# First routed layer: the up weights centred and split in two halves, ahead of the pages of the last two rounds, over four PSUM banks

## The reference, cut to what matters

```python
x = x + 0.5 * _L1_ffn_ref(_layernorm(x, axis=-1), L1_ffn_w_gate, L1_ffn_w_g, L1_ffn_w_u, L1_ffn_w_d)

def _L1_ffn_ref(x, w_gate, w_g, w_u, w_d):
    scores = x @ w_gate
    topk_scores, topk_idx = jax.lax.top_k(scores, K)
    topk_probs = jax.nn.softmax(topk_scores, axis=-1)
    gating = jnp.sum(jax.nn.one_hot(topk_idx, E, dtype=topk_probs.dtype) * topk_probs[..., None], axis=-2)
    hidden = jax.nn.silu(jnp.einsum('bsd,edm->ebsm', x, w_g)) * jnp.einsum('bsd,edm->ebsm', x, w_u)
    expert_out = jnp.einsum('ebsm,emd->ebsd', hidden, w_d)
    return jnp.einsum('bse,ebsd->bsd', gating, expert_out)
```

## Time and profile before

| | |
|---|---|
| median of 3 runs | 1740.12 us (1738.24 to 1742.35) |
| the profiled execution's own time | 1738.08 us |
| its span in the profile | 1735.6 us |
| mean granted TensorE clock | 0.884 of 2.4 GHz |
| busy, of the span | PE 84%, PEld 77%, DVE 76%, ACT 61%, POOL 62% |
| the first routed layer's rounds 2 and 3, arranging and up weights | about 838 to 909 us |
| its blocks | about 909 to 1115 us |

### The profile page before, as it was taken

How to read it: one execution, slowest core, us unless ns; L and a number is a source line. 1 busy time by engine, 2 the same in 40 slices (tenths; PEclk the granted TensorE clock), 3 DMA queues, 4 the chain that set the end, 5 groups by cost and what they waited for, 6 DMA issues and landing times.

```text
span 1735.6 us, 39578 instructions
## 1 busy us (share of the span) xinstructions
PE 1455.1 (84%) x10269; PEld 1333.8 (77%) x10269; DVE 1319.5 (76%) x4027; ACT 1053.3 (61%) x2639; POOL 1080.8 (62%) x1708
## 2 busy tenths in 40 slices
PE   8799999689948999998437999876999981289996
PEld 8589999667747999998316999875988861189995
DVE  7789999789988888888744777644788985367774
ACT  4588888444426888884214767574777730056674
POOL 7538887777733354533836666740788977746665
PEclk9999999899968999997567999955989975589998
DMA  6111010840001111002111222032222201122210
GB/s 195 50 38 32 32 35 13 190 111 1 0 6 55 35 33 36 31 8 107 46 52 47 67 64 54 20 105 64 86 74 78 82 15 47 56 62 65 65 51 9
DMA packets 93273, 96.25 MB, mean 55 GB/s; under 512 B 12072, under 2 KB 75709, under 8 KB 92576
## 3 DMA queue, kind: packets, MB, share of 16 engines
q1 hardware_dynamic: 83168, 76.70, 15.3%
q0 software_dynamic: 9920, 17.35, 3.0%
HBM read 63.75 MB, written 33.78 MB: 56 GB/s over the span
## 4 chain that ended last, share of the span: by engine, by line
PE 61%; issue 14%; DVE 12%; POOL 5%; ACT 4%; DMA 1%; another core or an unknown queue 1%; SPq 1%; DVEq 1%; POOLq 0%; ACTq 0%
PE banks L621 5%; PE banks L610 4%; PE banks L1300 4%; PE banks L1287 3%; PE banks L1322 3%; PE banks L1289 3%; PE banks L1288 3%; PE banks L601 3%; PE banks L603 3%; PE banks L602 3%; PE banks L1302 3%; PE banks L1301 3%; PE banks L622 2%; PE banks L1272 2%; PE banks L1273 1%
## 5 line engine op out<-in xcount | busy, mean ns | idle before, releaser
L1545 DVE TENSOR_TENSOR choice_hlo<-choice_h,choice_hhi 128x512 fp32r<-128x512 f32 x256 | 177.0, 732 | 22.8 <-ACT choice_hhi L1398 22.0
L1390 ACT ACTIVATE choice_h<-banks 128x512 f32<-128x512 f32 x256 | 152.4, 600 | 58.9 <-PE banks L1289 49.0
L892 DVE SCALAR_TENSOR_TENSOR top_h<-top_silu,top_xs,banks 128x176 f32<-128x176 f32 x364 | 128.5, 395 | 71.7 <-ACT top_silu L678 54.4
L933 POOL DMA_INDIRECT rt_rows<-X,top_slot x128 | 130.5, 1019 | 63.5 <-issue 37.8
L678 ACT ACTIVATE top_silu<-banks,top_xs 128x352 f32<-128x352 f32 x182 | 100.8, 554 | 102.7 <-PE banks L603 81.4
L1287 PE MATMUL banks<-choice_xin_hi,ec_w_hi 128*128 128x256 f32 x512 | 145.5, 284 | 4.8 <-ACT choice_xin_lo L1383 3.6
L1300 PE MATMUL banks<-choice_hhi,ec_w_hi 128*128 128x256 f32 x512 | 146.1, 285 | 3.4 <-DVE choice_hlo L1545 2.8
L1398 ACT ACTIVATE choice_hhi<-choice_h 128x512 fp32r<-128x512 f32 x256 | 146.6, 625 | 0.0
L1639 POOL TENSOR_SCALAR choice_y_hi_lo<-choice_yw 128x512 fp32r<-128x512 f32 x64 | 41.3, 645 | 164.9 <-ACT choice_yw L1413 163.8
L1288 PE MATMUL banks<-choice_xin_lo,ec_w_hi 128*128 128x256 f32 x512 | 143.6, 281 | 0.0
L1289 PE MATMUL banks<-choice_xin_hi,ec_w_lo 128*128 128x256 f32 x512 | 143.6, 280 | 0.0
(11 more groups left out here) (349 smaller groups left out, 5362.1 us busy)
## 6 DMA issues: line engine op xcount, KB each, us to landing
choice_token_row<-choice_tokens SPq DMA_DIRECT2D x64, 256.0 KB, 3.1
mlstm_run_row<-mlstm_run SPq DMA_DIRECT2D x32, 512.0 KB, 3.6
rt_rows<-rt_blank SPq DMA_DIRECT2D x2, 6188.0 KB, 38.3
top_xs<-rt_rows SPq DMA_DIRECT2D x182, 68.0 KB
X<-in_x SPq DMA_DIRECT2D x8, 512.0 KB, 6.9
ec_stage<-in_ec_w SPq DMA_DIRECT2D x2, 2048.0 KB, 12.8
X<-rt_y SPq DMA_DIRECT2D x8, 512.0 KB, 7.1
rt_rows<-X,top_slot POOLq DMA_INDIRECT x128
```

The costliest lines, as they stand in the source:

```text
L1545: dve.tensor_tensor(flat(self.hlo), self.h[:, c, :], flat(self.hhi).bitcast(F32), ALU.subtract).then_inc(self.hlo_done, 1)
```

## The change

The eight experts' chains are split into two halves and moved. TensorE computes experts 0 to 3 after the last scores and ahead of the ranks of round 2, and experts 4 to 7 behind those ranks and ahead of `arrange_sums`. ScalarE makes the high parts of experts 0 and 1 ahead of round 2's exponential and those of 2 to 7 behind it. VectorE makes the low parts of experts 0 to 3 behind round 2's `choose`, ahead of round 2's `page`, and those of 4 to 7 behind round 3's `choose`, ahead of round 3's `page`. There are four banks in place of two (6, 7, 0 and 1), so expert e waits for e-4.

```diff
-        self.pw = bk[6:8]
+        self.pw = (bk[6], bk[7], bk[0], bk[1])
...
         def centre_up(e):
             pe.wait_ge(w.split.loaded, 16 * (w.split.loads + len(w.parts)))
-            if e >= 2:
-                pe.wait_ge(sh.weights_lo, w.ups_from() + e - 1)
-            pe.matmul(self.pw[e % 2][:, 0:self.UP], w.centre[:, :], w.up[:, e, :], start=True, stop=True).then_inc(w.centred, 1)
+            need(pe, sh.weights_lo, w.ups_from() + e - 3 if e >= 4 else 0)
+            pe.matmul(self.pw[e % 4][:, 0:self.UP], w.centre[:, :], w.up[:, e, :], start=True, stop=True).then_inc(w.centred, 1)
 
         self.scores(pe, self.AHEAD[self.run], B)
         for r in range(self.CHOSEN_AHEAD[self.run], self.ROUNDS):
+            if not self.run and r == self.EARLY - 1:
+                for e in range(E // 2):
+                    centre_up(e)
             if r == self.EARLY:
+                if not self.run:
+                    for e in range(E // 2, E):
+                        centre_up(e)
                 self.arrange_sums(pe)
-                if not self.run:
-                    for e in range(E):
-                        centre_up(e)
             self.rank(pe, r)
...
+    def up_hi(self, act, first, last):
+        w = self.w
+        for e in range(first, last):
+            act.wait_ge(w.centred, e + 2)
+            act.activation(w.up_hi[:, e, :], self.pw[e % 4][:, 0:self.UP], ACT.Copy).then_inc(self.sh.weights_hi, 1)
+
+    def up_lo(self, dve, first, last):
+        sh, w = self.sh, self.w
+        for e in range(first, last):
+            dve.wait_ge(sh.weights_hi, w.ups_from() + e + 1)
+            dve.tensor_tensor(w.up_lo[:, e, :], self.pw[e % 4][:, 0:self.UP], w.up_hi[:, e, :].bitcast(F32),
+                              ALU.subtract).then_inc(sh.weights_lo, 1)
...
         for r in range(self.CHOSEN_AHEAD[self.run], self.ROUNDS):
-            if r == self.EARLY and not self.run:
-                for e in range(E):
-                    act.wait_ge(w.centred, e + 2)
-                    act.activation(w.up_hi[:, e, :], self.pw[e % 2][:, 0:self.UP], ACT.Copy).then_inc(self.sh.weights_hi, 1)
+            if not self.run and r == self.EARLY - 1:
+                self.up_hi(act, 0, 2)
             self.gate_exp(act, r)
+            if not self.run and r == self.EARLY - 1:
+                self.up_hi(act, 2, E)
...
-            if (r, part) == (self.EARLY, "choose") and not self.run:
-                for e in range(E):
-                    dve.wait_ge(sh.weights_hi, w.ups_from() + e + 1)
-                    dve.tensor_tensor(w.up_lo[:, e, :], self.pw[e % 2][:, 0:self.UP], w.up_hi[:, e, :].bitcast(F32),
-                                      ALU.subtract).then_inc(sh.weights_lo, 1)
+            if not self.run and (r, part) == (self.EARLY - 1, "page"):
+                self.up_lo(dve, 0, E // 2)
+            if not self.run and (r, part) == (self.EARLY, "page"):
+                self.up_lo(dve, E // 2, E)
             (self.choose_whole if part == "choose" else self.page)(dve, r)
```

## The result

The changed kernel takes 1730.99 us (median of 6 runs, 1725.16 to 1738.26) against 1740.88 us of the kernel before beside it (6 runs, 1730.85 to 1747.74). The ratio is 0.9941, with a 95% interval of 0.9914 to 0.9968: faster by 10 us, between 6 and 15. The forecast was 1728. Two later groups of runs, each beside the kernel before on one chip, gave the same kernel 0.9958 (0.9935 to 0.9982) and 0.9981 (0.9963 to 1.0000), so there is a gain, and it is rather 3 to 10 us than 12; the last of the three intervals just reaches no change. The profiled execution took 1730.98 us, its span is 1728.4 us (before: 1735.6).

A forecast was written before the change was run, and what follows sets the result against it. The stretch was taken as bound by a chain of waits, not a busy engine. Sends 18.9 us earlier, less a longer lag, gave 11.9 us off 1738.08, 1726.2; the median's 2.04 us above made it 1728, range 1719 to 1734.

The forecast's parts named there:

- Arranging to choice: VectorE's row between arranging and round 3's choice: the up weights' whole 19.78 us leave the path.
- First half: Experts 0 to 3, around round 2's ranks and page: ranks 0.9 us later, low parts hidden in VectorE's wait, ending at 856.3.
- the later 3.1 us of the old wait: VectorE's 5.19 us idle before round 2's page: ranks there after 2.1, the rest possibly with its own cause; 0.9 us charged.
- Second half: Experts 4 to 7, up to round 3's page: matmuls and high parts covered, low parts filling the ranks' wait, page at 882.9.
- a first send later than 895: Sign of being wrong at round 3's first send, forecast at 890.9: a later start would mean a pause on the path.
- What follows the sends: Last sends to seventh silu: sends end 18.9 us earlier at 910.8, silu at 927.0, 11.9 us earlier than before.
- the second layer's lag: Second routed layer: seventh silu 16.2 us after the last send, taken for the first layer in place of 9.2.
- the sum: Whole kernel: 11.9 us off the profiled 1738.08 us gives 1726.2, with a median forecast of 1728.
- The loads aren't held back: Rival, block loads beside the last sends: they go out unhindered, gaining 18.9 to 21.2 us, 1719 to 1721; chance 0.17.
- The pauses come along: Rival, ScalarE's high parts: 9.2 us of pauses fall on experts 0 to 3, leaving 2.7 us gained; chance 0.06.
- The slower rival: Block loads beside the sends starve at 5.7 us each, losing some 30 us, 1770; chance 0.03.

The follow-up runs named there:

- the hold in the kernel before: Kernel before, with GpSimd waiting ahead of round 2's fifth send until all eight low parts are there: 1734.13 us, ratio 0.9985.
- the sends paced: Changed kernel, with GpSimd sending 4 of the last round's 16 tiles at once and 12 one behind each block's work: 1730.59 us, ratio 0.9949.
- the held kernel: Changed kernel, with GpSimd waiting for round 2's ranks before round 1's fifth send: 1727.02 us, ratio 0.9970; timed again, ratio 0.9986.
- hold and pacing together: Changed kernel, with round 1's sends held from the fifth until round 2's ranks and 12 last-round sends paced behind blocks: 1729.74 us, ratio 0.9988.
- all in round 2: Changed kernel, with all eight low parts ahead of round 2's page and none ahead of round 3's: 1733.22 us, ratio 1.0011.

## Why the prediction was right or wrong

It was right that the kernel gets faster by more than can be told from no change, and the range holds the time. The size was forecast at 12 us and measured at 10, 7 and 3 in three groups. (The chances for "faster" add up to 0.90 and not 0.91: 0.72, 0.17 and half of 0.02.)

**Arranging to choice: right for the trace, too large for the kernel.** The 19.78 us left VectorE's path (873.28 to 873.20). But the term was read from one execution, and 9.8 us of it were pauses that another execution had only 1 us of there. The up weights' own cost is 9.98 us, shown by the hold in the kernel before.

**First half: right in place, wrong ahead of the page.** Low parts 0 to 3 ended at 854.32 (forecast 856.3). They follow VectorE's choice without a wait, and that came earlier because this execution was 1.8 us ahead from the slots of round 1 on. TensorE's ranks ended at 853.21 (forecast 857.2), for the same reason and because the granted clock was 1.00 over them, 2.4 GHz, where it had been 0.50, 1.2 GHz: their records took 1.80 us in place of 3.38. The text let the later 3.1 us of the old wait "have a cause of their own" and charged 0.9 us; the cause was there, and at 8.13 us it was longer than before. The page started at 862.46 in place of 860.3; counted from the slots of round 1 that is 4.0 us late.

**Second half: right.** High parts 4 to 7 came at 865 to 869, among late results, and nobody waited. Low parts ran at 880.25 to 882.06 (forecast 880.8 to 882.9). The missed term is the page behind them: the ranks ended at 878.73 + 3.28 = 882.01, and the page started at 886.14, 4.1 us later. So the first send came at 894.30 and not at 890.9, and the last ended at 914.20 and not at 910.8. The prediction named a first send later than 895 as a sign of being wrong. In two of the four profiles of the changed kernel it came later: at 900.20 in the execution whose slots of round 1 were 8 us late already, and at 901.78 where the pauses fell into the choice.

**What follows the sends: the number was right, the reason was wrong.** The seventh silu was forecast at 927.0 and came at 927.27. The step took the second layer's lag of 16.2 us, with three or four loads out before the last send. The DMA issues of the changed kernel, 893 to 914.2 us:

```profile
top_xs<-rt_rows SPq DMA_DIRECT2D x12, 68.0 KB
rt_rows<-X,top_slot POOLq DMA_INDIRECT x16
```

Twelve loads went out. The lag was 13.1 us, and what held the blocks was the third silu, from 901.4 to 917.2, by a late result of TensorE; with the sends paced this wait wasn't there. A held silu is nothing new either: in the kernel before the fourth came at 929.01, 12.0 us after its matmuls' end (916.64 + 0.32), among the sends. It was free 0.6 us ahead of the last send's end, the third silu now 3.0 us behind it, and that is nearly the whole difference between the lags of 9.2 and 13.1. That 927.0 was hit is luck: an error of 3.4 us in the sends' end and one of 3.1 us in the lag cancelled, and the 1.8 us that this execution was ahead hid under them. In the held kernel, whose sends have no gap where round 2's rows land, the DMA issues of 892 to 910 us are

```profile
top_xs<-rt_rows SPq DMA_DIRECT2D x4, 68.0 KB
rt_rows<-X,top_slot POOLq DMA_INDIRECT x15
```

and its lag is 927.00 - 910.25 = 16.7 us: there the second layer's few loads are seen, and the lag eats the 4 us that the hold had won. Late results have a share in it: the second silu came at 911.62, 6.2 us after its matmuls' end (904.88 + 0.50). The rule of the Trainium skill that DMAs of different engines interleave on the same engines (DMA: Bandwidth & Descriptors, "Issuing engines are not separate DMA queues") agrees with the twelve loads and doesn't tell of the four.

**What the sum left out.** From the seventh silu on, the forecast took the rest as unchanged. Busy time in the layer between the routed ones, first to last of its 32 sequences (us, PE, PEld, DVE, ACT, POOL, clock), in the kernel before once more and in the changed kernel:

```profile
1215.98:1420.65 204.67, 201.52 (x1614) 179.72 (x1609) 176.14 (x614) 143.90 (x435) 171.93 (x292) 0.91 0.20 71
```

```profile
1206.43:1414.91 208.48, 205.93 (x1621) 183.37 (x1613) 175.11 (x615) 143.49 (x435) 170.20 (x293) 0.89 0.20 69
```

The same work took 3.8 us longer, and TensorE, its bound, was busy 4.4 us longer at a lower granted clock, 0.89 against 0.91, a mean over stretches at 1.2 and at 2.4 GHz. This was so in all four profiles of the changed kernel (208.3, 208.5, 210.2, 210.9 us) and in neither of the kernel before (204.6, 204.7). The other two with the kernel before's order took 203.5 (four banks) and 201.5 us (held). Variants of the changed kernel lie on both sides: 203.0 for hold and pacing together, 204.6 for all in round 2, 206.7 for pacing, 208.5 and 208.2 for the hold, 208.8 without centring, with the same program in this layer. Why is open; no run was made that shifts this layer alone. It accounts for why 11.6 us at the seventh silu are 7.2 us in the span.

**The rivals.** "The loads aren't held back" came true in its premise and not in its time, since the late silu took the place of the loads. "The pauses come along" was right as a mechanism: pauses came at the pages, 8.1 and 4.1 us, where VectorE stood waiting, and at the high parts only where nobody waited. The one of 4.1 us is why the sends ended 3.4 us late. The slower rival's starving loads are seen in the two profiles of the held kernel (4 loads each beside the sends), and end with the sends.

## What to carry to other kernels

A wait in a chain has an owner: before a stretch is moved, split it into the work's own time and the pauses, by a second profile or by taking away what runs beside it. Here half of a stretch of 19.8 us was not the work that was moved, and other pauses came in its place. Two executions can also differ by several us before the stretch begins, here by up to 8, so read it from a mark at its start and not in absolute times. Work whose result can be late belongs where nobody wants it for longer than the pause: the second half was covered by 11 us and cost nothing, and with all eight pieces in front of one wait no gain was left that could be told.

## What was not expected of the hardware

While GpSimd's indirect DMAs follow each other every 1.26 us, a result of TensorE reached ScalarE or VectorE 3 to 16 us after the end that the trace gives for it: 9.2 us for the ranks, about 11 us for the fifth high part, 15.8 us for the third silu. It isn't every result (five high parts before, and those of 847 to 852 us in the changed kernel, came in time), its length changes from one execution to the next, and a gap of 3.4 us in the sends, or a send for each block in place of one each 1.26 us, made the wait it was aimed at vanish. In one execution VectorE's waits for its own last instruction were late too, by up to 1.7 us each and 11 us in one choice. Round 2's page was held for long only where centring matmuls stood around the ranks as well (4.1 to 9.2 us after the ranks' end, against 1.5 to 3.1). What carries the delay inside the chip wasn't found, and as the ends of matmuls are modelled, no run tells a late signal of TensorE from a late end of its work beside the sends. And loads that SyncE starts beside sends without a gap went out at 4 in 18 us, against 16 in 12.57 us with no sends.
